# Output-projection matmuls issued ahead of the FFN matmuls, in a selective-scan + FFN kernel on eight cores

## What is computed

```python
xn = _layernorm(x)                                    # x: 16384 x 1024
delta = softplus(einsum('btd,ed->bte', xn, Wd) + bd)
a_pos = softplus(a_log) + 0.0001                      # 1024 x 16
# per channel and 16 states, along the tokens:
state = exp(-delta_t * a_pos) * state + delta_t * b_param * xn_t ;  y_t = state.sum(-1)
attn = einsum('btd,ed->bte', y, Wo) + bo
real = einsum('bti,io->bto', xn, cos(theta + theta_noise))
imag = einsum('bti,io->bto', xn, sin(phi + phi_noise))
out  = x + attn + sqrt(real * real + imag * imag)
```

## Time and profile before

| | |
|---|---|
| median of 2 runs | 1110.67 us (1103.98 and 1117.36) |
| profiled execution, its own time | 1103.08 us |
| span of its slowest core (0), and of the others | 1101.4 us; 1093.0 to 1097.8 us |
| busy: TensorE, VectorE, ScalarE, GpSimd | 588.0, 818.8, 584.5, 152.4 us |
| mean granted TensorE clock, core 0 | 0.706 of full speed |
| projection stages, from the last scan on | 309.2 to 403.7, 661.0 to 782, 1026.7 to 1101.4 us |

### The profile page before, as it was taken

One profiled execution on the slowest core, in us unless ns is written; L12 is line 12 of the kernel. 1 busy time (PEld: TensorE's weight loads), 2 busy tenths in 40 slices (PEclk: granted clock), 3 DMA queues, 4 the chain that ended last, 5 costly groups with the idle time before them and its releaser, 6 DMA issues.

```text
span 1101.4 us, 9299 instructions; the slowest of 8 cores (1093.0 to 1101.4 us)
## 1 busy us (share of the span) xinstructions
PE 588.0 (53%) x2238; PEld 249.5 (23%) x2248; DVE 818.8 (74%) x721; ACT 584.5 (53%) x924; POOL 152.4 (14%) x127
## 2 busy tenths in 40 slices
PE   1323343445467545665565447656655665455785
PEld 1211011111123221221221114433212222021343
DVE  4279899999842449999999992434899999999423
ACT  5775767777633235666655553322466655565330
POOL 2477000000012100000000001221000000000232
PEclk9855556556668766667765668987766766666799
DMA  8777100000012310000000001241100000000023
GB/s 247 204 221 212 39 29 29 29 20 1 1 48 86 96 36 1 0 0 1 1 0 0 1 0 59 82 126 48 39 0 1 1 1 0 1 0 1 29 72 115
DMA packets 36324, 51.65 MB, mean 47 GB/s; under 512 B 3120, under 2 KB 19760, under 8 KB 36272
## 3 DMA queue, kind: packets, MB, share of 16 engines
q1 hardware_dynamic: 33584, 42.68, 13.2%
q0 software_dynamic: 2688, 8.39, 2.3%
HBM read 42.67 MB, written 8.39 MB: 46 GB/s over the span
## 4 chain that ended last, share of the span: by engine, by line
DVE 44%; PE 19%; issue 17%; ACT 16%; DMA 2%; DVEq 1%; SPq 0%; ACTq 0%; POOL 0%; POOLq 0%
DVE grot L845 37%; ACT abar L792 10%; PE pd L968 6%; PE pt L652 3%; PE pt L662 3%; DVE sfm L982 2%; ACT bdg_bf L177 2%; DMA xsub<-xin 1%; PE pe L380 1%; PE py L996 1%; DMA sfm<-xin 1%; PE pt L683 1%; DVE xsub L442 1%; PE py L380 1%; PE pt L380 1%
## 5 line engine op out<-in xcount | busy, mean ns | idle before, releaser
L845 DVE TENSOR_TENSOR_SCAN grot<-abar,gcar,vbuf 128x768 bf16<-128x768 f32 (+1 forms) x380 | 652.5, 1779 | 38.7 <-ACT abar L792 29.8
L792 ACT ACTIVATE abar<-delta,nega 128x768 f32<-128x768 f32 (+1 forms) x380 | 335.1, 896 | 238.3 <-DVE grot L845 235.5
L883 PE MATMUL pe<-grot,bdg_bf 128*128 128x384 bf16 x256 | 87.9, 439 | 115.0 <-DVE grot L845 114.9
L883 PE MATMUL py<-grot,bdg_bf 128*128 128x384 bf16 x256 | 84.5, 425 | 108.6 <-DVE grot L845 108.5
L295 PE MATMUL pd<-xnbf,wd_bf 128*128 128x384 bf16 (+1 forms) x368 | 98.5, 435 | 24.6 <-ACT xsub L318 14.8
L968 PE MATMUL pd<-ybf,wo_bf 128*128 128x384 bf16 (+1 forms) x318 | 74.7, 386 | 0.4 <-issue 0.4
L870 PE MATMUL py<-grot,bdg_bf 128*128 128x512 bf16 x62 | 33.4, 543 | 74.1 <-DVE grot L845 73.9
L726 POOL TENSOR_TENSOR xsub<-r,i 128x384 f32<-128x384 f32 (+1 forms) x9 | 18.1, 2011 | 381.0 <-ACT i L718 381.0
L870 PE MATMUL pe<-grot,bdg_bf 128*128 128x512 bf16 x61 | 33.0, 546 | 70.0 <-DVE grot L845 70.0
L295 PEld LDWEIGHTS pd<-xnbf,wd_bf 128*128 128x128 bf16 x368 | 47.8, 131 | 66.4 <-issue 56.9
L883 PEld LDWEIGHTS pe<-grot,bdg_bf 128*128 128x128 bf16 x256 | 19.0, 103 | 177.5 <-issue 175.6
(11 more groups left out here) (114 smaller groups left out, 669.0 us busy)
## 6 DMA issues: line engine op xcount, KB each, us to landing
xsub<-xin SPq DMA_DIRECT2D x14, 512.0 KB, 4.1
xres<-xin SPq DMA_DIRECT2D x32, 192.0 KB, 2.5
out<-osub POOLq DMA_DIRECT2D x32, 192.0 KB, 2.7
xres<-xin SPq DMA_DIRECT2D x8, 256.0 KB, 3.8
out<-osub POOLq DMA_DIRECT2D x8, 256.0 KB, 3.2
etmp<-tht SPq DMA_DIRECT2D x6, 256.0 KB, 5.3
r<-thn SPq DMA_DIRECT2D x6, 256.0 KB, 5.9
r<-pht SPq DMA_DIRECT2D x6, 256.0 KB, 4.0
```

The lines of the kernel that those rows point to most:

```text
L792: sx = run("scalar", lambda e, sl=sl_ab, par=par, dt=dt, n=n, tp=tp: e.activation(out=abar[:, sl * TP:sl * TP + tp], in_=delta[:, par * TP ...
L845: vs = run("vector", lambda e, g=gsl, sl=sl_ab, par=par, dt=dt, n=n, tp=tp: e.tensor_tensor_scan(out=grot[:, g * TP:g * TP + tp], data0=ab ...
L883: td = run("tensor", lambda e, c=c, g=gsl, dt=dt, n=n, bb=ypair[c]: e.matmul(bb[:, 0:384], bdg_bf[:, (dt * NST + n) * P:(dt * NST + n + 1) ...
```

## The change

The block that issues W(it), with its waits, stands at the head of the iteration, before F(it), instead of after `emit_ffn_chain`. `b = it % 2` moves with it. Nothing else changes: the lists of VectorE, ScalarE, GpSimd and SyncE keep their order.

```diff
             for it in range(nch):
                 dt, c0, wdth = cjobs[it]
+                b = it % 2
+                gd = grp_done[id(wo_bf)]
...
+                wait("tensor", "S", yev_last)
+                wait("tensor", "S", bfree_s.get(("pd", b), 0))
+                wait("tensor", "V", bfree_v.get(("pd", b), 0))
+                tw = None
+                for k in range(NDT):
+                    tw = run("tensor", lambda e, k=k, dt=dt, c0=c0, w=wdth, b=b: e.matmul(
+                        pd[b][:, 0:w],
...
                 if NFC + it < nch:
                     emit_ffn_mm(NFC + it)
                 if p + 1 < NPH:
...
                 if NFC + it < nch:
                     emit_ffn_chain(NFC + it)
-                gd = grp_done[id(wo_bf)]
...
-                wait("tensor", "S", yev_last)
-                wait("tensor", "S", bfree_s.get(("pd", b), 0))
-                wait("tensor", "V", bfree_v.get(("pd", b), 0))
-                tw = None
-                for k in range(NDT):
-                    tw = run("tensor", lambda e, k=k, dt=dt, c0=c0, w=wdth, b=b: e.matmul(
-                        pd[b][:, 0:w],
...
                 slot = it % 2
```

More of the change, by code:

```diff
@@ L937, in _build @@
                 dt, c0, wdth = cjobs[it]
+                b = it % 2
+                gd = grp_done[id(wo_bf)]
+                if isinstance(gd, tuple):
+                    wait("tensor", gd[0], gd[1])
+                else:
+                    wait("tensor", "G", gd)
+                wait("tensor", "S", yev_last)
[5 more added lines that the diff above has]
+                        pd[b][:, 0:w],
+                        wo_bf[:, k * 1024 + dt * P:k * 1024 + (dt + 1) * P],
+                        ybf[:, k * TP + c0:k * TP + c0 + w],
+                        start=(k == 0), stop=(k == NDT - 1)),
+                        "T" if k == NDT - 1 else None)
                 if NFC + it < nch:
```

## The result

The changed kernel takes 1065.55 us (median of 11 executions) against 1103.21 us before (10 executions); the ratio is 0.9639, 95% interval 0.9612 to 0.9666. It is 3.6% faster: 39.8 us by the ratio, 37.7 by the medians. The medians take in every execution, while the ratio leaves out one slow execution on each side (1117.36 and 1072.54 us). The forecast was 1061 us, in a range of 1046 to 1085.

A forecast was written before the change was run, and what follows sets the result against it. The projection stages were taken as bound by a chain between engines, chiefly VectorE's 102 us wait for W before sfm. Stage gains 7.5 + 16.2 + 18.4 = 42.1 us, off 1103.1, gave 1061 us, range 1046 to 1085.

The forecast's parts named there:

- Steady iterations: Iterations with F and no layer norm: sfm is done during F, so the period falls from 5.29 to 4.26 us.
- The loop through ScalarE and GpSimd: Squares to exponential, once per iteration: needs 4.16 us, just under TensorE's 4.26; as a rival bound, 4.8 us, 1069 us, chance 0.05.
- Head of a stage: Start of each projection stage: W(0) waits for the last ybf copy, at 1.2 GHz; +0.7, +0.35, -0.1 us in stages 3, 2, 1.
- Stage 3: Last projection stage: X(0) 0.7 us late, then 8 periods win 1.03 us each; -7.5 us.
- Stage 1: First projection stage: X(0) to X(7) falls from 76.40 to 57.8 us; -18.4 us after small corrections.
- Stage 2: Second projection stage: X(0) to X(12) falls from 92.97 to 75.6 us; -16.2 us after losses at its start and end.
- an unknown worth up to +13: Layer-norm iterations 1, 3 and 4: if the clock falls, five pay for slow transposes and following W and F; +13 us.
- a sign that the forecast is wrong: Layer-norm iterations: a transpose-heavy stretch at granted clock 0.50 reaching into the following F would show the forecast wrong.
- The load: xsub in layer-norm iterations: sfm ends 1.7 us before X(2), so the load comes in 2.1 us after X(2), taking 3.84.
- nothing but the stall: Rival: layer-norm iterations win only the sfm stall, since statistics stand behind osub on VectorE; gain 22, 1081 us, chance 0.10.
- the slow case: Rival: TensorE stays at 1.2 GHz through iterations with F, period 8.5 us; up to 1162 us, chance 0.03.
- Denser matmuls lower the granted clock: Rival: nearly 100% busy TensorE on eight cores loses clock in steady stretches, cancelling the period's gain; 1078 us, chance 0.10.

The follow-up runs named there:

- extra matmuls: The changed kernel plus matmuls that nobody reads, in TensorE's idle time in the layer-norm iterations: 1059.12 us, ratio 0.9591 to the kernel before.
- an expectation above: Expectation for the changed kernel with three layer-norm pieces moved one iteration later; that run measured 1062.27 us, ratio 0.9610 to the kernel before.
- The norm iterations alone: The kernel before, with W moved ahead of F and the layer-norm piece only in iterations that have such a piece: 1089.25 us, ratio 0.9872.

## Why the prediction was right, step by step

**What bounds the stages: right.** A chain between engines, whose main link was W before sfm: its wait fell from 102.0 to 33.0 us with every amount of work unchanged.

**Steady iterations: right.** Forecast 4.26 us, measured 4.23 in all eight cores; 5.62 for 512 tokens against 5.55. The loop through ScalarE and GpSimd costs nothing, but it was misread: the prediction gave it 4.16 us, the period of 5.29 less the idle 1.13 before the first square, and overlooked that ScalarE also waits for TensorE before the second:

```profile
1042.82 0.49 ACT L718 ACTIVATE i<-pt 128x384 f32<-128x384 f32 x1 [0.81 <-PE pt L662]
```

The loop needs about 5.29 - 1.13 - 0.81 = 3.35 us, and after the change the 0.81 is still there. It was never within 0.1 us of the bound.

**Head of a stage: right in its mechanism.** The new wait is 1.11 us, the stage starts at 1.2 GHz. Its price was put at +0.7, +0.35 and -0.1 in stages 3, 2 and 1; from the last scan to X(0) it is +0.6, +0.3 and -0.2 us in the 8-core mean.

**Stage 3: -7.5 forecast; -8.7 + 0.6 = -8.1 measured.** The periods of iterations 6 to 8 were 5.36 rather than 5.29, and the new one is 4.23.

**Stage 1: -18.4 forecast; -15.7 and +1.4 behind it.** The new length was right: 57.8 forecast, 58.3 measured. What was off is the length before. I took core 0's 76.4 us, and the mean of the cores is 74.0. The stretch behind stage 1 cost 1.4 us, all of it between X(7) and the first scan of the next scan stage, rather than the 0.3 put down for a slow X(7); with extra matmuls in iterations 6 and 7 it is back at 273.8, so this too is the clock.

**Stage 2: -16.2 forecast; -15.7 + 0.6 measured.** The terms didn't hold one by one. The step that failed is the sentence that TensorE's idle time before the transposes would be "too short to lose the clock". On core 5 the clock held through the transposes of iteration 1 and fell right after, though TensorE had stood idle only 1.23 us before them and 1.63 us before X. It had done little in that stretch (1.28 us busy in the 3 us from 655):

```profile
655.09 0.63 PE L380 MATMUL pe<-csts,xsub 128*128 128x128 f32 x4 [1.23 <-DVE xsub L442]
...
657.78 0.52 PE L997 MATMUL py<-csts,sfm 128*128 128x128 f32 x3 [1.63 <-DVE sfm L983]
...
658.14 2.72 PE L949 MATMUL pd<-ybf,wo_bf 128*128 128x384 bf16 x8
```

```profile
655.00:658.00 3.00, 1.28 (x10) 1.10 (x11) 1.81 (x3) 1.34 (x3) 0.00 (x0) 1.00 0.00 0
658.00:662.00 4.00, 4.00 (x17) 2.01 (x16) 1.18 (x2) 1.64 (x4) 1.72 (x2) 0.57 0.16 49
```

W(2) and the first matmuls of F(2) then ran at 1.2 GHz, so iteration 2 took 5.9 us instead of 4.26. So did those on the other seven cores (W(2) took 2.7 to 2.8 us on all). Likewise iteration 4, 9.0 instead of 7.7. Iteration 1 was 0.6 us longer than forecast for another reason, since it stays at 8.3 with the extra matmuls: from statistics to transposes it took about 4.4 us on most cores instead of 3.66. On the other side iterations 9 to 11 took 25.0 us instead of 26.0, since their transposes were fast in part of the cases. The prediction had the fall of the clock in iterations 1, 3 and 4 as an unknown worth up to +13 and took it at nothing, and it named a slow stretch that reaches into the following F as a sign that the forecast is wrong. That sign came. The run with extra matmuls puts the clock's cost in stage 2 at 6.4 us in the iterations that it shortened, 5.0 net; part of it, the slow iterations 9 to 12, was in the forecast.

**The load: half right.** It is issued 2 us before X(2), as forecast, but in iteration 3 of stage 2 it took 3.5 to 5.2 us until the statistics on the eight cores where 3.84 was assumed, and it ended last on all of them. In the mean the iteration is as forecast, 8.5 us against 8.6, while single cores have 7.8 to 9.5. (The 2.3 us in an expectation above had been taken from the issue of the load after it.)

**The rivals.** The norm iterations alone bring 14 us, so "nothing but the stall" is refuted. The loop didn't become the bound; it has 0.81 us to spare. The clock rose within the head of each stage in every core, so the slow case didn't come. "Denser matmuls lower the granted clock" is refuted for this execution of the changed kernel: TensorE is busy 29.00 of 29 us at 1.00, and all eight cores cover X(0) to X(8) of stage 3 in the same 33.8 us, at 1.00. It isn't refuted for every execution: in one of another kernel two cores did lose clock in this stretch (W early only in iterations without a norm piece).

```profile
1008.00:1037.00 29.00, 29.00 (x188) 18.55 (x187) 8.22 (x14) 14.12 (x28) 12.10 (x14) 1.00 0.30 93
```

Of the forecast 42.1 us the X starts show 38.5. The largest terms of the difference are the choice of core 0 as the basis in stage 1 (2.4 us), stage 2 (1.7, the clock above all) and the stretch behind stage 1 (about 1); stage 3 gave some of it back. That makes 3.6 us, where the forecast of 1061 and the measured 1065.55 lie 4.5 apart.

## What to carry to other kernels

On an engine that works in order, put work that something else waits for ahead of work that nobody waits for soon: the second then covers the first one's way through the other engines. Follow what the earlier result triggers in turn (here a load that a buffer held back): with W early only in iterations without a norm piece, iterations 1 and 3 of stages 1 and 2 became 11.5 us shorter, and the steady ones there 9.1. And when TensorE's work is packed more tightly, look at what is left between the packs: a stretch with a few transposes and two pauses of 1.2 and 1.6 us was enough to lose the clock, and matmuls that nobody reads won it back, 5 us here. Take the length "before" as a mean over the cores.

## What the runs showed of the hardware

- **A third value of the granted clock.** In one execution (W early only without norm pieces) cores 6 and 7 ran the dense stretch of stage 3 at a granted clock of 0.81 in many 4 us pieces, 0.85 in the mean, and took 4.4 and 5.2 us longer than the other six, cores 4 and 5 of the same die among them, which showed 1.00 while they ran the same matmuls. This speaks to the rule weighed in the prediction (the Trainium skill, TensorE: Matmul & The Clock Gate, Part 1, "The HAM clock gate"): the value of 13/16 agrees, 0.81, but it wasn't all of the die, and in the profiled execution of the changed kernel eight cores with dense matmuls for 34 us each didn't bring it on (each trace counts from its own core's start, so how far these stretches lie over one another isn't shown). What does bring it on stays open.
- **The clock falls without a long pause**, as above: on core 5, after 1.23 us idle, 1.1 us of transposes and 1.63 us idle, and in the same iteration on the other seven.
- **The time of one 512 KB load**, from the issue of `xsub` to its landing, was between 3.1 and 7.2 us in stages 1 and 2 of kernels whose queues have the same order. Two such loads and the residual's often stand in the same few us; which of them delays the other wasn't tried.
